# A two-layer attention and expert kernel: partial results stored in two halves of the partitions, the on-chip half laid out in pairs of groups, two takes shared out anew

## The reference

```
x = x + _L1_ffn_ref(_layernorm(x, axis=-1), ...)     # d = 256, 32 experts e, 4 sets s, inner size f = 32
grouped  = x.reshape(b, s // 32, 32, d)               # 128 groups n of 32 tokens t
logits   = einsum('bntd,des->bntes', grouped, Wc) + bc + tie
perm     = (logits == max over the 32 tokens)         # each of the 128 (e, s) picks one token of a group
permuted = einsum('bntd,bntes->bnesd', grouped, perm)
inner    = relu(einsum('bnesd,esdf->bnesf', permuted, W1) + b1)
result_p = einsum('bnesf,esdf->bnesd', inner, W2) + b2
result   = einsum('bnesd,bntes->bntd', result_p, perm)
```

## Time and profile before

| | us |
|---|---|
| median of 3 runs | 1939.19 (1938.2 to 1945.02) |
| the profiled execution's own time | 1944.29 |
| its span, first to last instruction | 1942.4 |
| gather steps and ups | about 1626 to 1740 |
| down rounds and stores | about 1740 to 1902 |
| return | about 1902 to 1942 |

### The profile page before, as it was taken

The page is one execution under the profiler, slowest core; times in us unless marked ns, Lnnn a source line. Parts: engine busy times, 40 slices in busy tenths (PEclk is TensorE's granted clock), DMA queues, the critical chain, the costliest instruction groups (busy, mean ns, idle before and its releaser), DMA issues.

```text
span 1942.4 us, 42261 instructions
## 1 busy us (share of the span) xinstructions
PE 1717.9 (88%) x16368; PEld 1470.4 (76%) x16368; DVE 1314.3 (68%) x2802; ACT 1153.3 (59%) x2882; POOL 822.2 (42%) x1292
## 2 busy tenths in 40 slices
PE   5899999999999999999997999999999999773235
PEld 4567676788999999999996787887887887662123
DVE  4798988427058988888866777777777766641124
ACT  1477776333467777777755777777777774331100
POOL 2244532100123333333316778888888775320000
PEclk7799999999999999999998999999999999875567
DMA  6756554368766666666765222222222111221117
GB/s 176 216 116 140 120 133 96 115 220 290 255 232 245 230 235 247 251 237 230 243 239 174 63 66 88 66 67 88 66 66 88 56 53 47 89 93 54 54 54 269
DMA packets 130553, 285.02 MB, mean 147 GB/s; under 512 B 13681, under 2 KB 74353, under 8 KB 116657
## 3 DMA queue, kind: packets, MB, share of 16 engines
q1 hardware_dynamic: 110768, 174.00, 29.4%
q0 software_dynamic: 19584, 108.31, 16.1%
HBM read 199.95 MB, written 82.05 MB: 145 GB/s over the span
## 4 chain that ended last, share of the span: by engine, by line
PE 70%; DMA 11%; DVE 10%; POOL 4%; issue 4%; ACT 1%; SPq 0%; DVEq 0%; POOLq 0%; ACTq 0%
PE ps L1250 11%; PE ps L1236 11%; DMA rp_scratch<-RPA 8%; PE ps L1928 5%; PE ps L373 4%; PE ps L219 4%; PE ps L1959 4%; PE ps L1914 4%; PE ps L1948 4%; PE ps L379 3%; PE ps L464 2%; PE ps L440 2%; DVE NM L592 2%; POOL P L209 2%; PE ps L540 2%
## 5 line engine op out<-in xcount | busy, mean ns | idle before, releaser
L196 ACT ACTIVATE P<-ps,NM 128x256 f32<-128x256 f32 x512 | 236.7, 482 | 126.5 <-DVE NM L185 125.8
L209 POOL TENSOR_TENSOR P<-P,RS 128x1024 f32<-128x1024 f32 x128 | 243.1, 1904 | 72.1 <-DVE RS L203 71.6
L1236 PE MATMUL ps<-XRP,W1P 128*128 128x256 f32 x1872 | 226.8, 281 | 3.3 <-DVE W1P L1319 3.3
L1236 PEld LDWEIGHTS ps<-XRP,W1P 128*128 128x128 f32 x1872 | 220.1, 190 | 3.6 <-DVE W1P L1319 3.6
L1250 PE MATMUL ps<-W2P,HP 128*128 128x256 f32 x1872 | 221.5, 277 | 0.0
L1250 PEld LDWEIGHTS ps<-W2P,HP 128*128 128x128 f32 x1872 | 218.0, 188 | 0.0
L592 DVE TENSOR_REDUCE NM<-ps 128x2 f32<-128x512 f32 x256 | 164.3, 684 | 33.4 <-PE ps L440 32.3
L690 ACT ACTIVATE PT<-ps 128x512 f32<-128x512 f32 x256 | 139.2, 597 | 66.3 <-PE ps L452 63.8
L185 DVE TENSOR_REDUCE NM<-ps 128x2 f32<-128x512 f32 x256 | 164.5, 684 | 5.7 <-PE ps L1914 4.2
L1170 POOL DMA_INDIRECT WE<-in_we,WIX x39 | 44.3, 1137 | 269.2 <-DVE W1P L1319 208.8
L1279 ACT ACTIVATE HF<-ps,WE 128x256 f32<-128x256 f32 x312 | 129.1, 465 | 43.0 <-PE ps L1236 43.0
(11 more groups left out here) (234 smaller groups left out, 3765.0 us busy)
## 6 DMA issues: line engine op xcount, KB each, us to landing
KS<-k_scratch SPq DMA_DIRECT2D x64, 256.0 KB, 3.1
V<-v_scratch SPq DMA_DIRECT2D x16, 1024.0 KB, 6.3
k_scratch<-KVM SPq DMA_DIRECT2D x52, 256.0 KB
QS<-q_scratch SPq DMA_DIRECT2D x96, 128.0 KB, 4.6
v_scratch<-KVM SPq DMA_DIRECT2D x40, 256.0 KB
ys_scratch<-YS SPq DMA_DIRECT2D x39, 256.0 KB, 7.9
ctx_scratch<-CHL SPq DMA_DIRECT2D x32, 256.0 KB, 3.0
CHR<-ctx_scratch SPq DMA_DIRECT2D x16, 512.0 KB, 4.5
```

The lines of the kernel that those rows point to most:

```text
L196: i = e.activation(self.P[u % 4][:, c, :], PS[SB[n % 3]][:, y * 256:y * 256 + 256], ACT.Exp, bias=self.NM[:, u % 4, c:c + 1], accum_out=se ...
L209: e.tensor_tensor(p, p, self.RS[:, u % 4, :].unsqueeze(2).to_broadcast([128, 4, 256]), ALU.mult).then_inc(self.s_pn, 1)
L1236: m = e.matmul(PS[p][:, hh * 256:hh * 256 + 256], W1P[i % 2][wi][:, cc * 1024 + hc * 128:cc * 1024 + hc * 128 + 128], XRP[i % 2][xi][:, cc ...
```

## The change

1. Each 1 MB store of a round becomes two of 512 KB, one for each block of 64 partitions. The bytes and their places in HBM stay the same; a round's semaphore now rises by 32.
2. `RPB` becomes `[128, 2, 32, 128, 2]`: two neighbouring groups lie beside each other, so the copies write pairs of elements (8 bytes), the pairs 1,024 bytes apart. The transposes of `turn_b` read every second element.
3. In the last two gathers (b = 14 and 15) ACT takes two banks and DVE two.
4. Both last weight loads, `WF2P[2]` and `[3]`, wait for all eight up parts.

```
+    def by_act(b):
+        return 3 if b < 14 else 2
...
-    RPB = Arena(nc, attn_at)("RPB", [128, 2, 64, 128], fp32)
+    RPB = Arena(nc, attn_at)("RPB", [128, 2, 32, 128, 2], fp32)
...
-            w.wait_ge(d_ks_rp[(k - 2) % 4], ks_sent + 16 * ((k - 2) // 4 + 1))
+            w.wait_ge(d_ks_rp[(k - 2) % 4], ks_sent + 32 * ((k - 2) // 4 + 1))
...
-        return (RPB[:, :, :, :].rearrange("p a g s -> p s (a g)")[:, es:es + 13:4, :],
-                PS[GATHER[r]][:, :].rearrange("p (q n) -> p q n", q=4))
+        return (RPB[:, :, :, :, :].rearrange("p a g s y -> p s (a g) y")[:, es:es + 13:4, :, :],
+                PS[GATHER[r]][:, :].rearrange("p (q n y) -> p q n y", q=4, y=2))
...
-                        m = e.transpose(PS[SMALL[t]][:, c0:c0 + 128], RPB[:, dh, 8 * i + 2 * t + u, :], ident)
+                        m = e.transpose(PS[SMALL[t]][:, c0:c0 + 128], RPB[:, dh, 4 * i + t, :, u], ident)
...
-            e.tensor_copy(px_part(b, 3), gathered(3)).then_inc(s_py, 1)
+            for g in range(by_act(b), 4):
+                e.tensor_copy(px_part(b, g), gathered(g)).then_inc(s_py, 1)
...
-            for k in range(3):
+            for k in range(by_act(b)):
...
-        w.wait_ge(s_u3, 5)
+        w.wait_ge(s_u3, 8)
         second(2)
-        w.wait_ge(s_u3, 6)
         second(3)
...
-            e.dma_start(rpd.rearrange("g (a k y) d -> k a g (y d)", a=2, k=8)[k],
-                        RPA[k % 2][:, :, :, :].rearrange("p h r d -> p (h r d)")).then_inc(d_ks_rp[k % 4], 16)
+            for a in range(2):
+                e.dma_start(rpd[:, 64 * a + 8 * k:64 * a + 8 * k + 8, :].rearrange("g y d -> g (y d)"),
+                            RPA[k % 2][64 * a:64 * a + 64, :, :, :].rearrange("p h r d -> p (h r d)")).then_inc(d_ks_rp[k % 4], 16)
```

More of the change, by code:

```diff
@@ L1559, in gather @@
             w.wait_ge(s_x3p, 2 * b + 2)
-            w.wait_ge(s_px, 3 * b)
-            w.wait_ge(s_py, b)
+            w.wait_ge(s_px, sum(by_act(c) for c in range(b)))
+            w.wait_ge(s_py, sum(4 - by_act(c) for c in range(b)))
             w.wait_ge(s_in, 7 if b == 8 else 0)
@@ L1596, in pe_up @@
             w.wait_ge(d_wf1[j], 16)
-        w.wait_ge(s_px, 24 * (hf + 1))
-        w.wait_ge(s_py, 8 * (hf + 1))
+        w.wait_ge(s_px, sum(by_act(c) for c in range(8 * hf + 8)))
+        w.wait_ge(s_py, sum(4 - by_act(c) for c in range(8 * hf + 8)))
         for q in range(8):
@@ L1890, in sp_tail @@
             w.wait_ge(s_e1, 2 * k + 1)
-            e.dma_start(rpd.rearrange("g (a k y) d -> k a g (y d)", a=2, k=8)[k],
-                        RPA[k % 2][:, :, :, :].rearrange("p h r d -> p (h r d)")).then_inc(d_ks_rp[k % 4], 16)
+            for a in range(2):
+                e.dma_start(rpd[:, 64 * a + 8 * k:64 * a + 8 * k + 8, :].rearrange("g y d -> g (y d)"),
+                            RPA[k % 2][64 * a:64 * a + 64, :, :, :].rearrange("p h r d -> p (h r d)")).then_inc(d_ks_rp[k % 4], 16)
         for j in range(4):
-            w.wait_ge(d_ks_rp[j], ks_sent + 16 * 2)
+            w.wait_ge(d_ks_rp[j], ks_sent + 32 * 2)
         w.wait_ge(s_fm, 16)
```

## The result

The changed kernel took 1825.72 us in the median of 4 runs (1824.05 to 1828.42), the kernel before 1942.11 in the 4 runs beside it (1938.2 to 1950.86). The ratio is 0.9396, with a 95% interval of 0.9359 to 0.9433: faster by 6.0%. The profiled execution took 1826.76 us (span 1824.9); before it was 1944.29 (1942.4).

The account below looks back on a forecast made before the run. RPA stores on two of sixteen DMA engines bound the kernel. From 1743.6 us, eight stores at 4.85 plus 1.6 end at 1784.0 instead of 1901.95: gain 118.0, median 1821.2 us, range 1810 to 1841.

Parts of the forecast that it names:

- (d): RPA stores: the split changes nothing, as memory addresses set the 53 GB/s limit; about 1939 us, chance 0.02.
- (e): RPA stores: each half-store sits on the same single engine, 39.6 us per 1 MB; about 2097 us, chance 0.01.
- 4.85 us: RPA stores: price of 1 MB from 64 partitions in steady flow, the middle of 2.7 and 7.0 us.
- The upper bound: RPA stores: 1 MB costs at most 7.0 us, from QS loads into 16 partitions at 144 GB/s.
- Rival (b): RPA stores: as slow as with 16 partitions, 7.0 us each; gain 100.8 us, total 1838.4, chance 0.13.
- Rival (a): Down rounds: full-rate stores, 2.7 us, hide under rounds of 4.3 us; gain 126.3 us, total 1812.9, chance 0.17.
- the low clock: Down rounds: if PE ran all at its low clock, 5.7 us a round, last store down at 1785.5.
- Part 2: Before the stores: takes shared with DVE save 0.4 us, later weight loads 3.1; moved loads delay store bytes to 1743.6.
- the third gap: Up parts: PE's 3.96 us pause, read as instructions waiting behind weight loads, shrinks to 0.85; 3.1 us saved.
- Part 3: RPB copies and transposes: pairs cost 1.37 us a round, save 1.1 without the stores' cover; transposes cost nothing extra.
- Rival (c): Return stage: transposes double in time, six steps of 1.97 us add 11.8; total 1833.0 us, chance 0.06.
- What would show it: New profile: DMA share 0.9 or more, about 200 GB/s, rounds 4 to 6 us; return over 41 us counts against.

Follow-up runs that it names:

- single groups: The changed kernel with RPB put back to its old layout, copies of single elements and transposes of neighbouring ones: 1832.22 us, ratio 0.9416.

## Why the prediction was right, and where only its sum was

**The cause was right.** Two engines of sixteen did the stores, by the first dimension of 2; with 64 they all did. The DMA share went from 0.13 to 0.81, and 150.3 us of waiting are gone. The split alone gives 0.9428, all the rest 0.9991. Rivals (d), no effect, and (e), one engine each, fell with the first window. Both kernels agree with the Trainium skill's rule on the engines ("DMA: Bandwidth & Descriptors", Why a DMA increments its semaphore by 16 and not by 1). The gain was forecast as 118.0 us and measured as 116.4 in the medians.

**The price of a store was near, but did not rule.** The term "4.85 us" is 4.5 for a store by itself and 4.1 where two in flight set the pace, both in this kernel's own rounds; only a queue kept full gets 3.1. The upper bound was worked out wrongly: 1.049 MB at 144 GB/s is 7.3 us and not 7.0, which would have moved the middle to 5.0. Rival (b), 7.0 us a store, was refuted. Rival (a), rounds set by PE, is what happened in kind, but neither its rate of 2.7 us a store nor its pace: "4.3 a round (3.6 at the high clock, some at the low)".

**The clock was mis-sized, and that the sum came out is luck.** I had the low clock only as an aside: 5.7 us a round, the last store down at 1785.5, "the sum hardly depends on it". Measured were 5.56 and 1782.9. The forecast's 1784.0 came by another road: 38.8 us for eight stores at 4.85. These were two candidate bounds 1.5 us apart, and the one I had not chosen ruled, since PE stayed at its low level through the rounds. The kernel with four added matmuls shows what the sum would have missed had the clock gone up: 7.6 us in this stage.

**Part 2.** From the ups to the first copy 2.9 us were saved, against the 3.1 said, but mostly by another mechanism. I had written "the third gap should shrink to the smallest of the three", from 3.96 to 0.85. It shrank to 2.04, the second went from 0.85 to 0.01, and 0.96 came up anew inside the first `down_a`. All gaps together gave 0.8 us in the two profiles. The other 2.1 are PE's clock, for which the prediction has no term here: 1.3 in the last piece of the ups, where it goes with the late loads in ten of eleven profiles, and 0.8 in the first piece, where it does not. My reason for all three gaps, instructions queued behind the loads, can hold for part of the third at most: 2.04 us of it were left with DMA at 4 to 8 GB/s. What PE stood for there stays open. The takes gave 0.3 each, not 0.2. Together the first copy came at 1736.79; I had said 1738.4. About 1.5 of the 5.1 us is neither loads nor takes: the earlier steps of this one execution were faster too. That the loads would push back the stores' bytes (1743.6) no longer mattered, because the stores were not the bound.

**Part 3.** The copies took 0.69 and 0.60 us as priced. I had "the pairs are hidden by the stores at the high clock", with 1.1 us a round if that cover went. The cover did go, and they saved 0.81 a round. They came out ahead of what they cost elsewhere, in the transposes. For these I took nothing, because "the weight load and the 128 columns stay as many". The count stays, but each weight load is 209 ns, not 141, and a step of 16 takes 2.12 to 2.19 us, not 1.97. So neither of the two reasons for a cost of nothing held. Over the eight steps it is at most 8 x 0.22 = 1.8 us. The return's +1.7 is not shown to be that: the return took 42.0, 40.9 and 41.3 us in the three profiles of the changed kernel, 42.9 with single groups, 39.8 with four added matmuls. It varies by more than the transposes explain. Rival (c), a doubling, fell.

**What would show it.** The share over the rounds is 0.81, not 0.9 or more; the 200 GB/s are there. The engines idle between stores because PE is not done. The rounds lie 5.56 us apart, within the 4 to 6. The waits before the copies to `RPA`, said to fall to some 10 us, are none for a store and 6.4 of DVE for PE. That the transposes would stay at 1.97 a step was wrong. That no gap of 4 us would be left in the ups was right. A return longer than 41 us had stood among the signs against; it is 42.0, and 40.9 the second time.

## What to carry to other kernels

When a transfer runs at 2 of 16 engines' share with each at its full rate, look at the first dimension of its pattern. That alone was worth 6% here, and no other part of the change was worth anything until it was done.

When a bound that large goes, work out the next two bounds side by side, PE's at both levels of its clock. Here they lay so near each other that the sum was right for the wrong one.

A transfer has no single price. The same 1 MB in two halves cost 4.5 us by itself and 3.1 in a full queue, at the same busy share, so say how many will be in flight before you price it. And compare gaps by their place in an engine's order, not by their number in a list.

## What the runs showed that I had not expected

- PE was busy in 35.00 of 35 us and had the low level, 1.2 GHz (granted clock 0.50). Its matmuls there are of 32 rows, 64 or 256 columns. Before it, in the last ups, the granted clock was 1.00. With four matmuls of 128 x 128 x 512 more in each round the granted clock was 1.00, and `down_b` fell from 3.62 to 1.94 us. Why the chip grants the low level there was not measured.
- The same program is granted different clocks in these rounds: 0.52 from the first copy to the first load back in the first two profiles, 0.58 in the third. The kernel with early loads had 1.00 in its first rounds.
- At the high level two stores in flight are few: the copies waited for them (7.09 and 7.97 us on the chain), and the rounds took 4.14 us. A third `RPA` buffer wasn't tried.
- A transpose whose operand steps by 8 bytes needs 68 ns more for its weight load, 209 for 141.
- Whole transfers from 128 partitions, mixed with halves, flowed at 298 GB/s (share 0.93), and halves alone at 340 (share 1.00), in one run each. One store of two halves by itself flowed at 226 to 235 (share 0.93 to 0.99).
